# Embedding stage: who does the first subtraction of the bf16 split for chunks 0 and 1

## What is computed

```python
fine = fine_embed_w[ids]                                    # 64 columns
dist = softmax(loc_to_cluster_w.T[ids] + loc_to_cluster_b)  # 64 clusters
h = concatenate([fine, dist @ coarse_embed_w])              # 128 columns
xn = silu(ln(layernorm(h)))
q, k, v = xn @ w_q + b_q, xn @ w_k + b_k, xn @ w_v + b_v
q, k = ln(q) * g_q + be_q, ln(k) * g_k + be_k
o = softmax(q k^T per head, 8 heads of 16) @ v
h = h + silu(o) @ w_o + b_o
h = h + ffn(layernorm(h))
```

```
part0 = bf16(full);  rest = full - part0;  part1 = bf16(rest);  part2 = bf16(rest - part1)
```

## Time and profile before

| | us |
|---|---|
| median of 3 runs | 1142.87 (1141.01 to 1144.10) |
| the profiled execution | 1141.88 |
| its span, first to last instruction | 1140.0 |
| first matmul of the attention stage, from the span's start | 237.68 |

### The profile page before, as it was taken

One profiled execution on the slowest core, in us unless ns is written; L12 is line 12 of the kernel. 1 busy time (PEld: TensorE's weight loads), 2 busy tenths in 40 slices (PEclk: granted clock), 3 DMA queues, 4 the chain that ended last, 5 costly groups with the idle time before them and its releaser, 6 DMA issues. The chain is left out here.

```text
span 1140.0 us, 29425 instructions
## 1 busy us (share of the span) xinstructions
PE 1002.7 (88%) x12048; PEld 528.8 (46%) x12048; DVE 918.5 (81%) x1792; ACT 789.2 (69%) x1518; POOL 205.3 (18%) x317
## 2 busy tenths in 40 slices
PE   0586677559999999999999999999999985899998
PEld 0474566403444434444434334344434423677876
DVE  3667876888889999998989889889898823789974
ACT  1557768404787887887878778787788794576763
POOL 7668755430000000000000000000000000111100
PEclk9987777856999999999999999999999997899999
DMA  3123956460252242342342342342320024243011
GB/s 77 62 85 103 206 111 189 150 139 3 42 94 39 52 84 39 57 79 40 61 75 40 58 78 39 58 78 40 60 55 12 14 95 136 67 135 99 28 38 38
DMA packets 81341, 84.15 MB, mean 74 GB/s; under 512 B 23985, under 2 KB 58358, under 8 KB 81206
## 3 DMA queue, kind: packets, MB, share of 16 engines
q1 hardware_dynamic: 79158, 78.07, 31.0%
q0 software_dynamic: 2048, 4.20, 1.5%
HBM read 47.73 MB, written 34.08 MB: 72 GB/s over the span
## 5 line engine op out<-in xcount | busy, mean ns | idle before, releaser
L1139 DVE TENSOR_REDUCE b_neg_max<-psM 128x1 f32<-128x1024 f32 x512 | 603.3, 1220 | 71.2 <-PE psM L1037 67.9
L1111 ACT ACTIVATE prob<-psS 128x512 f32<-128x512 f32 x1024 | 529.0, 603 | 160.5 <-PE psS L1057 160.5
L1037 PE MATMUL psM<-ks,qs 96*32 96x512 bf16 x4096 | 414.6, 393 | 18.6 <-PEq L900 14.8
L1057 PE MATMUL psS<-qs,ks 99*32 99x512 bf16 x4096 | 403.7, 382 | 10.1 <-ACT prob L1111 4.5
L1071 PE MATMUL psO<-prob,vs 128*17 128x512 f32 x2048 | 266.2, 592 | 0.2 <-ACT prob L1111 0.2
L1057 PEld LDWEIGHTS psS<-qs,ks 99*32 99x32 bf16 x4096 | 113.3, 96 | 213.9 <-ACT prob L1111 100.7
L1037 PEld LDWEIGHTS psM<-ks,qs 96*32 96x32 bf16 x4096 | 112.7, 97 | 177.4 <-DVE b_neg_max L1139 80.4
L932 POOL CAST mpart<-b_neg_max 128x16 bf16<-128x16 f32 x32 | 6.3, 196 | 639.0 <-DVE b_neg_max L1139 625.9
L1071 PEld LDWEIGHTS psO<-prob,vs 128*17 128x17 f32 x2048 | 59.2, 98 | 52.3 <-ACT prob L1111 1.1
L1350 ACT ACTIVATE hid<-c_psU,b_sb 128x512 f32<-128x512 f32 x64 | 43.9, 688 | 46.1 <-PE c_psU L1423 46.1
L322 POOL DMA_INDIRECT emb<-in_table,idx x64 | 65.5, 1023 | 19.8 <-issue 14.6
(11 more groups left out here) (133 smaller groups left out, 949.9 us busy)
## 6 DMA issues: line engine op xcount, KB each, us to landing
qk_parts<-qk_part SPq DMA_DIRECT2D x48, 256.0 KB, 2.7
qs<-qk_parts SPq DMA_DIRECT2D x192, 64.0 KB, 3.6
ks<-qk_parts SPq DMA_DIRECT2D x96, 128.0 KB, 4.2
o_cols<-ot SPq DMA_DIRECT2D x32, 256.0 KB, 4.3
qs<-mpart_t SPq DMA_DIRECT2D x384, 1.0 KB, 1.7
v_rows<-vrow SPq DMA_DIRECT2D x16, 272.0 KB, 2.3
vs<-v_rows SPq DMA_DIRECT2D x8, 544.0 KB, 6.2
h_rows<-h SPq DMA_DIRECT2D x16, 256.0 KB, 5.1
```

Of the source, the lines that this page charges most:

```text
L1037: last = nc.tensor.matmul(psM[count % MRING][q * HP:(q + 1) * HP, n, :], qs[buf][0:DATA_ROWS, half, hh, at + q * HP:at + (q + 1) * HP], ks ...
L1057: last = nc.tensor.matmul(psS[unit % SRING][q * HP:(q + 1) * HP, :], ks[buf][0:ROWS, GH * gb + hh, tile * P + q * HP:tile * P + (q + 1) * HP],
L1111: nc.scalar.activation(prob[step % PRING][:, hh, :], psS[unit % SRING][:, :], ACT.Exp).then_inc(score_free, 1)
L1139: nc.vector.tensor_reduce(neg_max[e % 2][:, unit:unit + 1], psM[count % MRING][:, :, :], AX.XY, ALU.max, negate=True).then_inc(max_free, 1)
```

## The change

Passes 0 to 2 only. The subtraction rest = full - part0 for chunks 0 and 1 is taken off POOL and given to DVE. On DVE the one for chunk 0 stands between `stats_front(it+1, (2, 3))` and `stats_back(it, 2)`, the one for chunk 1 between `aggregate_back(it, 2)` and `silu(it+1, 0)`. POOL keeps chunks 2 and 3. A new semaphore, `first_rest_done`, counts DVE's two per pass, and `round_rest` waits on it for chunks 0 and 1; the counts of `rest1_done` are renumbered to POOL's two per pass.

```diff
@@ POOL, end of a pass
                     if it < 2:
                         regather(*later.pop(0))
-                    if not last:
-                        subtract_part0(it, 0)
-                        subtract_part0(it, 1)
                     if it == 0:
                         regather(*later.pop(0))
                     subtract_part0(it, 2)
@@ DVE
+                def subtract_part0(r, w):
+                    dve.wait_ge(part0_done, use(r, w))
+                    nc.vector.tensor_tensor(rest[w], full[w][:, :, :], part[0][w][:, :, :], ALU.subtract).then_inc(first_rest_done, 1)
@@
                         stats_front(it + 1, (0, 1))
                         stats_front(it + 1, (2, 3))
+                    if not last:
+                        subtract_part0(it, 0)
                     stats_back(it, 2)
                     aggregate_back(it, 2)
+                    if not last:
+                        subtract_part0(it, 1)
                     if not last:
                         silu(it + 1, 0)
                         silu(it + 1, 1)
@@ ACT
                 def round_rest(r, w):
-                    act.wait_ge(rest1_done, use(r, w) - (SLOTS if r == ITERS - 1 else 0))
+                    if w < SLOTS:
+                        act.wait_ge(first_rest_done, r * SLOTS + w + 1)
+                    else:
+                        act.wait_ge(rest1_done, r * SLOTS + w - SLOTS + 1)
                     nc.scalar.activation(part[1][w][:, :, :], rest[w], ACT.Copy).then_inc(part1_done, 1)
```

More of the change, by code:

```diff
@@ L284, in embed @@
         rest1_done = sem("rest1_done")
+        first_rest_done = sem("first_rest_done")
         rest_by_dve = sem("rest_by_dve")
```

## The result

The change makes the kernel faster: median 1135.08 us of 6 runs (1132.73 to 1137.22) against 1144.37 of 6 (1141.01 to 1144.74) on the same chip. The ratio is 0.9929, with a 95% interval of 0.9917 to 0.9942, so 0.71% or 8.1 us. The forecast of 1137.2 was 2.1 us too high, and the range held the time.

The account below looks back on a forecast made before the run. It took DVE's chain at the turns of the embedding passes, held by POOL's subtractions, as the bound. Gains of 3.5 + 0.4 + 1.8 = 5.7 us off the median 1142.87 gave 1137.2 us, range 1133.0 to 1141.8.

Parts of the forecast that it names:

- The stage's end moves everything: At the barrier before attention (first matmul 237.68 us): what the embedding stage saves or loses moves the end by as much.
- Middle of a pass: DVE's two new subtractions there, 2.3 us of work, cost 0.1 us, covered by idle time before the second silu.
- POOL's delay: Mid-pass, DVE's new subtractions hold POOL's small instructions and gather issue: 0.7 us in pass 0, 0.9 in pass 1.
- Turn 0 to 1: From pass 0 to pass 1: short logits, L450 still held by POOL's pair but ending earlier; 3.5 us gained.
- Turn 1 to 2: From pass 1 to pass 2: L388 held under POOL's pair, the wait before subtract_part1 gone; 0.4 us gained.
- Turn 2 to 3: From pass 2 to pass 3: L435 no longer held by POOL, the chain behind it earlier; 1.8 us gained.
- Half clock counted as 0: PE's half-clock projections at turn 0 to 1: less idle might give back up to 3.4 us; counted as 0.
- Held for one: Rival: DVE's instruction gets in after the first of POOL's pair; gain 9.4 us, time 1133.5; chance 0.15.
- The gathers pay: Rival: in passes 0 and 1 new subtractions hold POOL fully, gather-to-logits 2.4 us late; gain 2.5, time 1140.4; chance 0.22.
- DVE is the bound: Rival: DVE's 6.8 us of new work finds no cover, turns give nothing back; 1149.7 us, slower; chance 0.06.
- The wait changes its name: Rival: ACT waits for PE in place of POOL, L388 is held in every turn; 1140.1 us; chance 0.07.

Follow-up runs that it names:

- e2: The changed kernel with the second subtraction of POOL's pair (chunk 3) waiting on a semaphore for the first (chunk 2), in all passes; ratio 0.9921.
- e8: The changed kernel with a third DVE subtraction of the same form per pass, into tiles nobody reads; ratio 0.9937.
- e1: The changed kernel with POOL still running two same-shape subtractions in the old place, on scratch tiles, ACT not waiting for them; 1146.7 us, ratio 1.0045.
- e4: The changed kernel with DVE's subtraction for chunk 0 moved behind the statistics of chunk 2, beside that for chunk 1; ratio 0.9934.
- b2: The kernel before the change, unedited, traced a second time; span 1140.3 us, first attention matmul at 240.19 us.

## Why the prediction was right, point by point

The mechanism held at the first and the third turn and failed at the second. Part of the closeness in time is luck: the forecast of 1137.2 subtracts 5.7 from the median of 3 runs (1142.87), and the median of 6 was 1144.37, from which the same 5.7 gives 1138.7. One of the prediction's own signs of being wrong came true, the short L388 of the second turn (1.29 where about 3 was forecast). The others did not: DVE's waits for POOL behind A stayed at 0.8 or less, and the attention began at 231.43. ACT's wait for POOL's subtraction fell from 18.5 to 3.6, as forecast.

- *The stage's end moves everything.* Right: what was gained by pass 3 is what the timing shows, within the scatter named above.
- *Middle of a pass: 2.3 us of work for 0.1.* In pass 0 the second silu began about 88.07 (second of the two from 87.47), 0.4 later than before after the setup is set aside (87.56 + 0.15). The idle 1.51 of the earlier trace rows was the cover, as said; it cost 0.4 where 0.1 was forecast. A waited 0.81 for ACT's part0, a little longer than forecast.
- *POOL's delay, 0.7 and 0.9.* It was 1.0: `root_back(0,2)` at 90.89 against 89.74 less 0.15 of setup. `norm_back(0,2)` started 1.0 late (92.61), with 0.78 of waiting for it. Right mechanism, a term too small by 0.3.
- *Turn 0 to 1, 3.5.* It was 3.8. The landing at 101.11 (forecast 101.0), L386 at 0.43, statistics at 105.02 (104.95) and L448 let go at 110.2 (110.35) all came as worked out.
- *Turn 1 to 2, 0.4.* This is the term that was mis-sized: it was 2.3. I let L386 be held for both subtractions, because L388 had been in every pair of the earlier trace rows. There the second subtraction was ready long before the first began. Here part0 of chunk 3 was done only about 146.1, after the first had started at 145.32, and L386, asking at 146.44, took 1.29 and got in between. The bound I gave for that case was 2.1. e2 shows by itself that a second subtraction that isn't ready when the first starts lets DVE in. The third turn of the kernel before shows it too: POOL's pair began at 196.66, part0 of chunk 3 came at about 197.5, and the L461 at 198.51 took 1.37, against 1.21 free.
- *Turn 2 to 3, 1.8.* It was 1.5. L433 took 0.69, as forecast.
- *Half clock counted as 0.* TensorE ran the projections of pass 1 earlier and at full clock (granted 1.00 from 99 to 105 us, against 0.52 in the earlier trace rows), and in the changed kernel this gave nothing beyond the turn's 3.8, as assumed, since POOL held DVE until 110.2. What I hadn't counted is pass 3, where single executions of one kernel differ by up to 2.4 us at different granted clocks.
- *Rivals.* "Held for one" was right in turn 1 and wrong in turn 0 (2.79 again); as a whole it forecast 9.4 and 1133.5, which is nearer to the timed 8.1 and 1135.08 than my own 5.7 and 1137.2. It was given 0.15 and the forecast 0.50. "The gathers pay" (1140.4) is out: the delay was real but 1.0 in place of 2.4. "DVE is the bound" (slower by 6.8) is refuted by the result itself, and by e8. "The wait changes its name": it did (ACT now waits 40.3 us for PE, 31.0 before), and e1 shows that taking away its wait for POOL brings nothing as long as POOL still holds DVE.

The Trainium skill's "SBUF — State Buffer" (Who interferes with whom) has the lock go to whoever starts first, for the whole of one instruction. The traces agree with the first half. They differ on the second: 5.01 us under three and 7.08 under four POOL instructions in a row for the same L388. They also differ on descriptor writing, which that section infers to be untouched by such DVE instructions: the issue took 1.20 under B and 1.94 in e4, where it began just after B did, against 0.94. The warning of the Trainium skill's "Perfetto Trace Analysis" (Optimizing Scalar/DVE Operations), that moving work between these two might not help, didn't come true for this move: it helped because POOL's instructions stopped holding DVE's.

## What to carry to other kernels

Where two engines share a port, look at short instructions that last much longer than their like (here 2.95 in place of 0.43 us): the profile books that as busy time, so no view of waits shows it. Before you read a wait as the cost, leave the wait out and keep the suspected holder; here losing the wait (14.85 us on ACT) brought nothing while the holder stayed. A move of work pays by where its instructions stand on the other queue: half of this one gave nothing in time that could be told from zero, all of it gave 0.7%.

## What the runs showed of the hardware that was not expected

- DVE's 0.43 us L388 was held for as many POOL subtractions in a row as stood there: 2.93 under two, 5.01 under three, 7.08 under four. A wait of POOL's second instruction for its first cut an L450's like from 2.79 to 0.70 us, for 0.14 us more of POOL's time. The scalar_tensor_tensor L435 got in after one in every case (2.53, 2.54, and 1.47 when it asked 1.2 us into the pair).
- An indirect transfer's issue on POOL that began under a DVE subtraction of an f32 and a bf16 tensor ended some 0.8 us after that instruction: it took 1.20 us when it began 0.8 us into it, and 1.94 and 2.03 when it began with it (under B in e4, and under the second L463 after the change), in place of 0.94.
- TensorE's granted clock over the same stretch of the kernel before averaged 0.76 in one execution and 0.60 in another (b2), and the stretch was 2.4 us longer in the second. Differences under that need a mark ahead of such a stretch, or many runs.
